# Down products of seven hidden tiles in three rounded passes, in a macaron feed-forward and attention block

## The reference, cut to what matters

```python
x = x + 0.5 * ffn(layernorm(x))
x = x + attn(layernorm(x))        # attn itself adds its input: x + x_n + out @ Wo
x = x + 0.5 * ffn(layernorm(x))

# ffn: 32 experts of 64 hidden values, 16 anchors of 32, one shared of 64
scores = sigmoid(x @ gate_weight.T)              # picks 2 of 4 groups, then 6 experts of 32
g, u   = x @ w_gate, x @ w_up                    # every expert is computed for every row
h      = silu(g) * u                             # hidden values
out    = (cw * h) @ w_down                       # cw: the weight of each expert for each row
out   += shared + 0.1 * anchor                   # same form; the anchor's weight is one-hot
```

## Time and profile before

| | |
|---|---|
| median of 3 runs | 1445.76 us (1445.65 to 1445.84) |
| the profiled execution | 1446.04 us |
| its span, first to last instruction | 1444.0 us |
| TensorE busy | 1408.9 us, 98% |
| VectorE busy | 1111.9 us, 77% |
| ScalarE busy | 800.4 us, 55% |
| GpSimd busy | 289.4 us, 20% |
| mean granted TensorE clock | 0.999 |

### The profile page before, as it was taken

The page is one execution under the profiler, slowest core; times in us unless marked ns, Lnnn a source line. Parts: engine busy times, 40 slices in busy tenths (PEclk is TensorE's granted clock), DMA queues, the critical chain, the costliest instruction groups (busy, mean ns, idle before and its releaser), DMA issues.

```text
span 1444.0 us, 27512 instructions
## 1 busy us (share of the span) xinstructions
PE 1408.9 (98%) x9680; PEld 964.9 (67%) x9680; DVE 1111.9 (77%) x2521; ACT 800.4 (55%) x1909; POOL 289.4 (20%) x586
## 2 busy tenths in 40 slices
PE   5999999999999999999999999999999999999998
PEld 4666666666656667666766666676666666666665
DVE  8888888887677777777777787778867777787775
ACT  4344344433357777777878777777644333323322
POOL 1000000000124444444434444443400000000000
PEclk9999999999999999999999999999999999999999
DMA  6443333333300000000000000000043434333332
GB/s 232 163 131 106 113 98 124 105 113 102 118 31 2 2 2 2 2 2 2 2 2 2 2 2 2 2 2 2 2 127 105 121 109 127 106 125 111 119 113 87
DMA packets 59025, 98.07 MB, mean 68 GB/s; under 512 B 6160, under 2 KB 15504, under 8 KB 58896
## 3 DMA queue, kind: packets, MB, share of 16 engines
q1 hardware_dynamic: 58896, 96.38, 21.3%
HBM read 92.68 MB, written 3.67 MB: 67 GB/s over the span
## 4 chain that ended last, share of the span: by engine, by line
PE 86%; DVE 7%; ACT 3%; issue 2%; POOL 0%; DMA 0%; SPq 0%; POOLq 0%; DVEq 0%; ACTq 0%
PE banks L424 19%; PE banks L199 14%; PE banks L201 13%; PE banks L200 13%; PE banks L562 10%; PE banks L527 7%; PE banks L548 5%; PE banks L383 2%; PE banks L537 2%; DVE nmax L1310 2%; ACT work L867 1%; PE banks L395 1%; DVE q_lo L1299 1%; DVE ctx_lo L1330 1%; DVE stage L1325 1%
## 5 line engine op out<-in xcount | busy, mean ns | idle before, releaser
L777 ACT ACTIVATE work<-banks 128x512 f32<-128x512 f32 x320 | 191.1, 598 | 445.1 <-PE banks L201 434.2
L424 PE MATMUL banks<-work,wd 128*128 128x512 f32 x672 | 342.9, 593 | 0.6 <-DVE work L1188 0.4
L1197 DVE TENSOR_TENSOR work<-banks,work 128x512 f32<-128x512 f32 x320 | 220.9, 691 | 150.5 <-ACT work L777 146.0
L867 ACT ACTIVATE work<-banks,nmax 128x512 f32<-128x512 f32 (+3 forms) x512 | 264.8, 529 | 52.0 <-DVE nmax L1310 48.0
L1471 POOL TENSOR_SCALAR work<-work,rrec 128x512 f32<-128x512 f32 (+3 forms) x512 | 264.0, 539 | 0.0
L199 PE MATMUL banks<-xT_hi,wg_hi 128*128 128x512 f32 x336 | 248.2, 739 | 0.4 <-DVE wu_lo L1179 0.4
L1188 DVE TENSOR_TENSOR work<-work 128x512 f32<-128x512 f32 x320 | 226.8, 709 | 5.5 <-DMA work<-cw_rows 1.2
L1310 DVE TENSOR_REDUCE nmax<-banks 128x2 f32<-128x1024 f32 (+3 forms) x256 | 195.7, 807 | 3.1 <-PE banks L537 3.1
L1325 DVE COPY stage<-banks 128x1024 f32<-128x1024 f32 (+1 forms) x128 | 122.0, 953 | 53.6 <-PE banks L548 53.4
L424 PEld LDWEIGHTS banks<-work,wd 128*128 128x128 f32 x672 | 126.1, 189 | 35.2 <-DVE work L1188 4.1
L201 PE MATMUL banks<-xT_hi,wg_lo 128*128 128x512 f32 x336 | 133.4, 397 | 0.0
(11 more groups left out here) (140 smaller groups left out, 2183.3 us busy)
## 6 DMA issues: line engine op xcount, KB each, us to landing
work<-cw_rows SPq DMA_DIRECT2D x320, 256.0 KB, 3.1
x<-in_x SPq DMA_DIRECT2D x8, 256.0 KB, 6.4
out_rows<-x SPq DMA_DIRECT2D x8, 256.0 KB, 2.2
cw_rows<-cwT SPq DMA_DIRECT2D x16, 96.0 KB, 1.9
stage<-in_w_gate SPq DMA_DIRECT2D x3, 448.0 KB, 5.1
wd<-in_w_down SPq DMA_DIRECT2D x3, 448.0 KB, 7.4
stage<-in_w_up SPq DMA_DIRECT2D x2, 448.0 KB, 6.0
stage<-in_wq SPq DMA_DIRECT2D x1, 512.0 KB, 3.8
```

The lines of the kernel that those rows point to most:

```text
L424: pe.matmul(psY, wd[:, j * P:(j + 1) * P], z[part_slot(j)], start=j == 0, stop=j == HT - 1, skip_group_check=True).then_inc(s["down_ps"], 1)
L777: nc.scalar.activation(silu[j % 2], psG[j % 3], ACT.Silu).then_inc(s["silu_done"], 1)
L867: m = nc.scalar.activation(prob[:, p % 2, i, o:o + w], ps[:, i, so:so + w], ACT.Exp, bias=nmax[:, p % 2, i, qb:qb + 1], accum_out=rsum[:, ...
L1197: tt(gated[j % 3], psU[j % 3], silu[j % 2], ALU.mult).then_inc(s["gated_done"], 1)
```

## The change

Down products of tiles 0 to 4, 18 and 19 (`SPLIT_Z`) run through `mm3` in three fp32r passes; `split_z` leaves out chunk 0, and tiles 18 and 19 of chunks 7 and 15. For each such tile ScalarE copies z into a high part (`z_high`, after silu of the next tile), and GpSimd subtracts it from z for the low part (`z_low`). The parts use rings of four slots that lie in the attention's q and k buffers. The w_down tiles are stored in a new order, the seven first, and their high and low parts are made once in chunk 0 (ScalarE in loop 10, then GpSimd). Tiles 0 to 4 of w_down have no full copy any more beside the staging tile, from which chunk 0 reads them; attention's weights are loaded over it after chunk 0's five products. Several scratch tiles of the routing share memory, and cw has 48 columns a row tile instead of 128, so its padding isn't set to zero any more. Statistics of input rows move from loops 3 and 4 to 6 and 9, their root on ScalarE from loop 8 to 12.

The diff, cut to its core:

```diff
...
 HP = H // 2
+SPLIT_Z = [0, 1, 2, 3, 4, 18, 19]
 KB_OFF = [0, 4 * P, 7 * P, 9 * P]
...
 GT = HT // W_GROUPS
+DOWN_ORDER = SPLIT_Z + [j for j in range(HT) if j not in SPLIT_Z]
 
...
         wu = [sb(f"wu_{n}", [P, HC - P], F32R) for n in ("hi", "lo")]
-        wd = sb("wd", [P, HC])
+        wd = sb("wd", [P, HC - 5 * P])
+        wd_parts = [sb(f"wd_{n}", [P, GT * P], F32R) for n in ("hi", "lo")]
         stage = sb("stage", [P, 2, 3, GT * P])
...
         score = sb("score", [P, TB, E])
-        sc = sb("sc", [P, TB, E])
+        sc, chosen = [stage_flat[:, 4 * PW + i * TB * E:4 * PW + (i + 1) * TB * E]
+                      .rearrange("p (t e) -> p t e", t=TB) for i in (0, 1)]
         t4 = [sb(f"t4_{i}", [P, TB * G, 4]) for i in range(2)]
...
         gscore = sb("gscore", [P, TB * G, 1])
-        gcmp = [sb(f"gcmp_{i}", [P, TB, G, G]) for i in range(3)]
-        grank = sb("grank", [P, TB * G, 1])
-        gpen = sb("gpen", [P, TB * G, 1])
+        gcmp = [t[:, :, :].rearrange("p (t a) b -> p t a b", t=TB) for t in t4] + \
+            [sb("gcmp_2", [P, TB, G, G])[:, :, :, :]]
+        grank, gpen = t1[0], t1[1]
         masked = sb("masked", [P, TB, E])
...
         onehot = sb("onehot", [P, TB, E, TOPK])
-        chosen = sb("chosen", [P, TB, E])
-        wts = sb("wts", [P, TB, E])
+        wts = masked
         wsum = sb("wsum", [P, TB, 1])
...
         anch = sb("anch", [P, TB, L])
-        cw = sb("cw", [P, TB, P])
+        cw = sb("cw", [P, TB, ROWS])
         cwT = sb("cwT", [ROWS, CH])
...
         qk = [[sb(f"{m}_{n}", [P, 2, CH], F32R) for n in ("hi", "lo")] for m in "qk"]
+        z_parts = [[t[:, i, :] for t in qk[n] for i in (0, 1)] for n in (0, 1)]
         ctx_parts = [sb(f"ctx_{n}", [P, CH], F32R) for n in ("hi", "lo")]
...
         spread_loads = [sem(f"s_spread{k}") for k in range(NSPREAD)]
+        wd_split_hi, wd_split = sem("s_wd_split_hi"), sem("s_wd_split")
         wsplit_hi = [sem(f"s_wsplit_hi{k}") for k in range(W_GROUPS)]
...
             return tiles(g, j) - (HT if j == HT - 1 else 4 if j > 3 else 5)
+
+        def splits(g, j):
+
+            return (g - 1) * len(SPLIT_Z) + SPLIT_Z.index(j) + 1 - (2 if g >= NC else 0)
+
+        def split_z(g, j):
+
+            return j in SPLIT_Z and g != 0 and not (j > 4 and g in (NC - 1, 2 * NC - 1))
+
+        def down_columns(j):
+
+            return slice(DOWN_ORDER.index(j) * P, (DOWN_ORDER.index(j) + 1) * P)
 
...
                 cols = slice(k * GT * P, (k + 1) * GT * P)
-                sp.dma_start(wd[:, cols], wd_in[:, cols]).then_inc(wd_loads[k], 16)
+                if k == 0:
+                    sp.dma_start(stage[:, 0, 2, :], wd_in[:, cols]).then_inc(wd_loads[k], 16)
+                    cols = slice(5 * P, cols.stop)
+                sp.dma_start(wd[:, cols.start - 5 * P:cols.stop - 5 * P], wd_in[:, cols]).then_inc(wd_loads[k], 16)
 
...
                 sp.wait_ge(wsplit[k], 2)
+            sp.wait_ge(wd_split, 1)
+            sp.wait_ge(s["down_ps"], 5)
             for w, src in enumerate((wq_in, wk_in)):
...
                 pe.wait_ge(s["route"], (g + 1) * ROUTE)
-                to_columns(ps, cw).then_inc(s["cwT_ps"], 1)
+                to_columns(ps[0:ROWS, :], cw).then_inc(s["cwT_ps"], 1)
 
...
             def down(g, j, first):
-                pe.wait_ge(s["z_done"], tiles(g, j))
+                c = down_columns(j)
                 if j == 0 and not first:
                     pe.wait_ge(s["y_evac"], g)
-                if first and g == 0 and j % GT == 0:
-                    pe.wait_ge(wd_loads[j // GT], 16)
-                pe.matmul(psY, wd[:, j * P:(j + 1) * P], z[part_slot(j)], start=j == 0,
+                if split_z(g, j):
+                    pe.wait_ge(s["z_lo"], splits(g, j))
+                    if g == 1 and j == 0:
+                        pe.wait_ge(wd_split, 1)
+                    mm3(pe, psY, [w[:, c] for w in wd_parts], [t[splits(g, j) % 4] for t in z_parts],
+                        j == 0, False).then_inc(s["down_ps"], 1)
+                    return
+                pe.wait_ge(s["z_done"], tiles(g, j))
+                if first and g == 0:
+                    pe.wait_ge(wd_loads[DOWN_ORDER.index(j) // GT], 32 if j in SPLIT_Z else 16)
+                weights = stage[:, 0, 2, c] if j < 5 else wd[:, c.start - 5 * P:c.stop - 5 * P]
+                pe.matmul(psY, weights, z[part_slot(j)], start=j == 0,
                           stop=j == HT - 1, skip_group_check=True).then_inc(s["down_ps"], 1)
...
 
+            def z_high(g, j):
+                act.wait_ge(s["z_done"], tiles(g, j))
+                nc.scalar.activation(z_parts[0][splits(g, j) % 4], z[part_slot(j)], ACT.Copy) \
+                    .then_inc(s["z_hi"], 1)
+
             def split_hi(k, ws=range(2)):
...
                         prep_sigmoid(g + 1)
-                    if 0 < g < NC - 2 and j == 8:
+                    if 0 < g < NC - 2 and j == 12:
                         row_std(g + 2)
...
                         y_copy(g - 1)
+                    if setup and j == 10:
+                        act.wait_ge(wd_loads[0], 32)
+                        nc.scalar.activation(wd_parts[0][:, :], stage[:, 0, 2, :], ACT.Copy) \
+                            .then_inc(wd_split_hi, 1)
+                    if split_z(g, j - 1):
+                        z_high(g, j - 1)
                 if first:
...
                 at_stats, at_mean = (10, 11) if last else (19, 20)
-                at_input_stats = 18 if setup else 3
+                at_input_stats, at_input_mean = (18, 19) if setup else (6, 9)
                 after_attention = g0 == NC and first
...
                         rows_stats(g + 2)
-                    if g < NC - 2 and j == at_input_stats + 1:
+                    if g < NC - 2 and j == at_input_mean:
                         rows_mean(g + 2, input_stats(g + 2))
...
 
-            nc.vector.memset(cw[:, :, ROWS:], 0.0)
             nc.vector.memset(z[part_slot(HT - 1)][0:MI, :], 0.0)
...
                 split_lo(2, w)
+            pool.wait_ge(wd_split_hi, 1)
+            nc.gpsimd.tensor_tensor(wd_parts[1][:, :], stage[:, 0, 2, :], f32(wd_parts[0][:, :]),
+                                    ALU.subtract).then_inc(wd_split, 1)
             pool.wait_ge(s["small_loaded"], 16)
+
+            def z_low(g, j):
+                pool.wait_ge(s["z_hi"], splits(g, j))
+                nc.gpsimd.tensor_tensor(z_parts[1][splits(g, j) % 4], z[part_slot(j)],
+                                        f32(z_parts[0][splits(g, j) % 4]), ALU.subtract) \
+                    .then_inc(s["z_lo"], 1)
+
+            for g in range(NC - 1):
+                for j in SPLIT_Z:
+                    if split_z(g, j):
+                        z_low(g, j)
+            for j in SPLIT_Z[:5]:
+                z_low(NC - 1, j)
 
...
                 norm(n, 1)
+
+            for g in range(NC, 2 * NC):
+                for j in SPLIT_Z:
+                    if split_z(g, j):
+                        z_low(g, j)
 
...
         "w_up": hidden_columns(L0_ffn_w_up, L0_ffn_anchor_w_up, []),
-        "w_down": down.reshape(HT, P, D).transpose(1, 0, 2).reshape(P, HT * D),
+        "w_down": down.reshape(HT, P, D)[DOWN_ORDER].transpose(1, 0, 2).reshape(P, HT * D),
         "gate_weight": np.asarray(L0_ffn_gate_weight).T,
...
```

## The result

The changed kernel takes 1441.1 us (median of 7 runs, 1439.5 to 1442.8), the kernel before 1445.76 (7 runs beside them). The ratio is 0.9966, 95% interval 0.9956 to 0.9976: 0.34% faster, some 4.7 us. Timed again later it took 1440.1 (5 runs, 1438.6 to 1443.0; ratio 0.9963, 0.9949 to 0.9976). The profiled execution took 1440.4, its span is 1438.6. The forecast was 1433.4 with a range of 1429 to 1441: the sign was right, but 4.7 of the 12.4 us came, and the median lies just outside the range. The executions of the changed kernel lie 3 to 4 us apart.

The account below looks back on a forecast made before the run. The prediction took TensorE's work (98% busy) as the bound: 16.7 us saved less waits of 1.1, 0.3, 0.6 and 2.3 gave 12.4, so 1445.76 would become 1433.4 us. The range was 1429 to 1441.

Parts of the forecast that it names:

- Three passes save 0.165 us: Split down products: three passes 0.697 us against a full product's 0.865; 101 products save 16.7 us, ends 15.9 and 17.3.
- The subtraction takes 1.24 us: GpSimd's subtraction for the low part of z, 512 columns: 1.24 us each, ends 1.0 and 1.81.
- Rival 2: GpSimd's subtraction takes 1.4 to 1.5 us, so boundaries and entries cost 9 of 16.7 us: 1438 us, chance 0.14.
- (a): Chunk boundaries: tile 19's subtraction delays tile 20's constant multiplication; 0.22 us in five stage 1 chunks, 0.05 in six of stage 3.
- Chunk 9, put at 0.05: Boundary into chunk 9, counted among six stage 3 chunks at 0.05 us each, range 0 to 0.17.
- (b): Chunk 1, first one split: tile 0's late z, copy and subtraction make TensorE wait 0.6 us; 0 if GpSimd is first.
- (c): Chunk 8, after attention: tile 0's copy and subtraction make its down product 2.3 us late, ends 1.7 and 2.9.
- Costed at nothing: Moved statistics, chunk 0's split of down weights, 128 KB more loads, attention's later weight load, scratch and cw changes: 0 us.
- Rival 3: GpSimd and VectorE become the bound, subtraction and multiplication taking 2.41 us a loop: 1458.6 us, chance 0.06.
- Rival 1: Nothing waits, GpSimd gets in ahead or the product after attention finds its part ready: 1429.1 us, chance 0.13.

Follow-up runs that it names:

- experiment 1: Changed kernel without GpSimd's 101 subtractions, each split product using z's high part twice, ScalarE's copies kept: 1432.5 us, ratio 0.9908.
- Experiment 5: Changed kernel, but in chunk 8 ScalarE takes the square root of the statistics ahead of tile 19's high part: 1439.65 us, ratio 0.9956.
- experiment 10: Changed kernel with tiles 17 and 18 split in place of 18 and 19: 1437.5 us, ratio 0.9943.
- Experiment 4: Changed kernel, but attention's four weight loads (2 MB) issued after chunk 1's spread loads, not ahead of its store of routing weights: 1438.25 us, ratio 0.9940.
- experiments 6: Changed kernel, but in steady chunks VectorE normalises the rows ahead of tile 20's constant multiplication of the chunk before: 1439.7 us, ratio 0.9948.
- Experiment 8: Kernel before, but chunk 8's first down product also waits for z of tile 2, a TensorE standstill of 2.5 us: 1450.0 us, ratio 1.0028.
- (7): Changed kernel with the moved statistics put back in loops 3, 4 and the root behind loop 8: 1440.7 us, ratio 0.9956.

## Why the prediction came out too low

The prediction failed at what it put at nothing or next to nothing: the root behind tile 19's high part in chunk 9, the granted clock behind chunk 8's wait, and the loads of attention's weights ahead of chunk 1's store. Its chain at the boundaries was right and came out too short. By its own steps:

- **Three passes save 0.165 us.** Right within 3%: 0.160, so 16.2 us and not 16.7. (Its terms as printed, 0.865 less 0.697, give 0.168, and 17.0 us.) On the page "FP8 and Floating Point Precision" of the Trainium skill, section "TensorE Precision Notes", a product is four passes, which by estimate would have given 0.216; the trace says 0.160.
- **The subtraction takes 1.24 us.** 1.27 to 1.29 when free. Its mean is 1.44 to 1.46, as it waits for VectorE too. Rival 2 named this term, but 1.4 to 1.5 is not its own length.
- **(a) The boundary: 0.22 x 5 + 0.05 x 6 = 1.4.** Measured 0.47 x 5 + 0.20 x 5 = 3.35, and chunk 9 1.5. In stage 1 the forecast had tile 19's subtraction end 5.04 us after tile 19's silu starts, and it did; it had the transposes due at 6.40, and they were. The instruction that is held is another one, the small copy and not the constant multiplication, and the normalisation ends 0.14 later for it; 0.06 from VectorE's end to TensorE's start and 0.06 behind the transposes weren't in the sum. In stage 3 the constant multiplication is the one held (1.56), and the loss of 0.20 lies 0.03 above the forecast's upper end.
- **Chunk 9, put at 0.05 like the others.** Here the failed step is an order and not only a block: ScalarE's root for chunk 9 stands behind tile 19's high part, which waits for z of tile 19. It starts 5.1 us after tile 19's silu in place of 3.5. With the subtraction left out (1) 0.8 of the 1.5 us stay; the rest is the small copy held ahead of that z (0.79 in place of 0.17) and what follows. Experiment 5 moved the root and gained 0.4, experiment 10 took the high part and the subtraction away and gained 1.1.
- **(b) Chunk 1: 0.6.** Measured 1.66, by the table; 0.9 in another profile of the same kernel. The step "attention's weights, whose load now waits for five down products done long before" failed: their transfers stand ahead of the store that chunk 1 waits for, in both kernels. Before, slack hid it. Experiment 4 removes all of it.
- **(c) Chunk 8: 2.3.** The wait was 2.12, right. The term that was missing is the granted clock behind it, 1.5 us in this profile. I took the clock for 1.00 throughout because the windows of before showed it so; they left out the first chunk. There the trace of before has the low level from 25.1 to 28.5 us (window below the list), behind pauses of 2.64 and 1.38 us. How often it falls in chunk 8 isn't settled: with a standstill of over 2 us there three of eight profiles have it (the changed kernel, the root's and the normalisation's run), without one none of ten. Experiment 8 doesn't decide it.
- **Costed at nothing.** The statistics: right (7). The setup: 0.5 us more, by 0.2 at the first pass and 0.3 in chunk 0. This need not be the change's: chunk 0 took 56.29 to 56.84 us in the profiles of the changed kernel and its versions, and 56.25 and 56.39 in the two of the kernel before.

The first chunk of the kernel before, columns as in rows 3 with the clock third from the end:

```profile
25.10:28.40 3.30, 3.30 (x10) 2.63 (x9) 3.17 (x5) 0.66 (x2) 0.00 (x0) 0.50 0.30 88
```

The sum of what was mis-sized: 0.5 for the products, 2.0 for the boundaries of the steady chunks, 1.5 for chunk 9, 1.1 for chunk 1, 1.6 for chunk 8, 0.5 for the setup: 7.2 us, less 0.2 for attention and chunk 7. The profiled execution is 6.8 above the 1433.6 that the sum gave for it. Rival 3 (GpSimd and VectorE the bound) was wrong: steady loops keep their pace. Rival 1 asked what would happen if nothing waits, and experiment 1 comes closest, at 1432.5 and not 1429.1.

On the page "SBUF — State Buffer" of the Trainium skill, section "Who interferes with whom", VectorE's one-input instructions in a two-port mode are excluded as fully as two-input ones. The trace agrees, on more instructions than I used it for: 0.42 became 1.56 us, and the normalisation 1.12 became 2.13.

## What to carry to other kernels

When an operation moves to GpSimd, list every VectorE instruction that can fall into its time, small ones and one-input ones too, and look in a trace for which of them are held; give each of those the rest of GpSimd's instruction, and look at which stands ahead of something TensorE waits for. Ask the same of the engine that got the copy: what now stands behind it in order, and what does it wait for? A product's saving is safe, its added latency is paid wherever a pipeline fills (after a stage change, behind a transfer), so price the entries one by one and look at what else queues ahead of the transfer. Where a wait of one or two microseconds is added in front of TensorE, allow for the clock behind it, and try first to put other products there.

## What the runs showed of the hardware

- GpSimd's two-input instruction on 512 columns takes 1.27 to 1.29 us when nothing is in its way. A VectorE instruction that starts inside it may be held until its end even when it is four numbers wide (0.17 became 0.83) or takes one input (0.42 became 1.56, 1.12 became 2.13).
- Others aren't held. In the changed kernel 33 products read from PSUM and one SBUF tile, 52 statistics instructions (BATCH_NORM) and 13 copies of one number a partition start inside a subtraction and keep their 0.69, their 0.16 or 0.28, and their 0.14 to 0.15 us; so does the reciprocal in experiments 5 and 10 (0.30 and 0.17).
- The granted clock drops to the 1.2 GHz level for 3.4 us behind a pause of TensorE in some executions of the same program and not in others: at 1055 behind 2.12 us, at 1038 (experiments 6 and 7) behind pauses of 0.79 and 0.70 that every profile has. In the first chunk every profile has it, for 3.4 or 6.8 us, behind pauses of some 2 to 3 and 0.9 to 1.4 us. One drop costs 1.5 to 1.6 us: chunk 8 takes 54.40 in place of 52.86, sixteen small products 3.94 in place of 2.37.
- The mean granted clock sorts the executions of the kernel before: of 39 beside the experiments, the nine of 1447.2 us and more have 0.996, the other thirty (1445.5 to 1446.8) 0.997 to 0.999. Where in them the clock fell, no profile shows.
- A 96 KB store that takes 2.0 us took 5.5 to 7.6 us from its issue to the next issue that waits for it, with 2 MB of loads ahead of it.
